# Decoder of two layers on one Trainium2 core: the value products of a self-attention unit issued in one block instead of two halves

## What is computed

```python
q = split_heads(_binlinear(x, Wq, bq))
k = split_heads(_binlinear(x, Wk, bk))
v = split_heads(_binlinear(x, Wv, bv))
att = jnp.einsum('bhtd,bhsd->bhts', q, k) * scale
att = jax.nn.softmax(att, axis=-1)
y = jnp.einsum('bhts,bhsd->bhtd', att, v)
y = y.transpose(0, 2, 1, 3).reshape(B, T, C)
return _binlinear(y, Wp, bp)
```

## Time and profile before

| | |
|---|---|
| median of 3 runs | 2285.22 us (2285.04 to 2290.65) |
| profiled execution, its own time | 2289.26 us |
| its span, first to last instruction | 2287.7 us |
| self-attention of layer 0, first to last step of the main stream | about 85 to 560 us |
| self-attention of layer 1, the same | about 921 to 1315 us |
| PE busy over the span | 76% |
| DVE busy | 60% |
| ACT busy | 47% |
| POOL busy | 37% |
| value products, L948 | 2048 records, 226.4 us busy |

### The profile page before, as it was taken

How to read it: one execution, slowest core, us unless ns; L and a number is a source line. 1 busy time by engine, 2 the same in 40 slices (tenths; PEclk the granted TensorE clock), 3 DMA queues, 4 the chain that set the end, 5 groups by cost and what they waited for, 6 DMA issues and landing times. The chain is left out here.

```text
span 2287.7 us, 35514 instructions
## 1 busy us (share of the span) xinstructions
PE 1738.8 (76%) x12206; PEld 875.7 (38%) x12222; DVE 1382.0 (60%) x3734; ACT 1080.9 (47%) x1482; POOL 841.4 (37%) x862
## 2 busy tenths in 40 slices
PE   4888888888688865677777745666656887999992
PEld 2122222222355542233333322323323554666661
DVE  2667777773478972566666543535447875555554
ACT  2366766766367962555555411121214563444441
POOL 3235554522477313577776430000002342222221
PEclk8589999999699986799998666668777998999996
DMA  4333332320100003344433014112112333222217
GB/s 95 61 66 61 58 62 50 49 27 1 67 1 1 1 4 56 53 63 57 56 48 48 2 28 58 25 35 38 37 30 95 124 121 106 63 61 61 59 53 234
DMA packets 117853, 126.58 MB, mean 55 GB/s; under 512 B 21684, under 2 KB 104116, under 8 KB 117652
## 3 DMA queue, kind: packets, MB, share of 16 engines
q1 hardware_dynamic: 106980, 101.94, 22.7%
q0 software_dynamic: 6480, 18.23, 2.1%
q10 hardware_dynamic: 4224, 4.19, 0.6%
HBM read 77.94 MB, written 45.16 MB: 54 GB/s over the span
## 5 line engine op out<-in xcount | busy, mean ns | idle before, releaser
L655 ACT ACTIVATE at_pexp<-ps 128x1024 f32<-128x1024 f32 (+3 forms) x480 | 385.8, 826 | 200.5 <-PE ps L888 199.4
L716 DVE TENSOR_REDUCE at_mx<-ps 128x1 f32<-128x512 f32 x512 | 324.0, 683 | 146.3 <-PE ps L895 144.3
L895 PE MATMUL ps<-at_ks,at_qs 48*128 48x512 f16 (+3 forms) x1024 | 291.6, 359 | 95.6 <-DVE at_mx L716 42.4
L182 PE MATMUL ps<-mo_wall,mo_xt 128*128 x1704 | 302.0, 327 | 1.1 <-DVE mo_xt L2316 0.6
L888 PE MATMUL ps<-at_qs,at_ks 50*128 50x512 f16 (+4 forms) x1024 | 253.8, 346 | 29.1 <-DMA at_qs<-at_mhl 23.2
L948 PE MATMUL ps<-at_pexp,at_vaug 128*32 128x512 f32 (+4 forms) x2048 | 226.4, 536 | 7.4 <-issue 6.3
L182 PEld LDWEIGHTS ps<-mo_wall,mo_xt 128*128 128x128 f16 x1704 | 161.1, 98 | 95.2 <-issue 4.3
L2073 POOL DMA_INDIRECT mo_yd<-mo_xn,mo_idu x71 | 68.1, 959 | 272.1 <-DVE mo_xn L2335 266.9
L718 DVE CUSTOM_DVE_ANT_0 at_junk<-ps,at_lmask 128x192 bf16<-128x192 f32 x384 | 115.4, 352 | 80.7 <-PE ps L895 79.6
L895 PEld LDWEIGHTS ps<-at_ks,at_qs 48*128 48x128 f16 x1024 | 75.4, 98 | 213.3 <-DVE at_mx L716 122.6
L888 PEld LDWEIGHTS ps<-at_qs,at_ks 50*128 50x128 f16 x1024 | 70.7, 98 | 174.6 <-issue 88.5
(11 more groups left out here) (397 smaller groups left out, 3873.2 us busy)
## 6 DMA issues: line engine op xcount, KB each, us to landing
at_qs<-at_scratch SPq DMA_DIRECT2D x96, 128.0 KB, 7.2
at_ks<-at_scratch SPq DMA_DIRECT2D x96, 128.0 KB, 7.8
mo_xr<-mo_xs SPq DMA_DIRECT2D x71, 136.0 KB, 2.3
at_scratch<-at_qkh SPq DMA_DIRECT2D x64, 128.0 KB
at_scratch<-at_qkl SPq DMA_DIRECT2D x64, 128.0 KB
x_qs<-x_qscratch SPq DMA_DIRECT2D x48, 128.0 KB
mo_stage<-in_m_gate SPq DMA_DIRECT2D x9, 512.0 KB, 3.7
mo_stage<-in_m_up SPq DMA_DIRECT2D x9, 512.0 KB, 4.6
```

The costliest lines, as they stand in the source:

```text
L182: last = nc.tensor.matmul(out, lhs, rhs, start=(n == 0), stop=(n == len(terms) - 1))
L655: last = act.activation(columns(pexp[:, U % 2, hh], at, n, stride, width), columns(banks(r, ST[S % 2], 2), at, n, stride, width), ACT.Exp, ...
L716: last = ve.reduce_max(out, score, AX.X)
L895: return nc.tensor.matmul(banks(r, MX[i % 2])[:, piece.at:piece.at + piece.n], qs[rows, (n // 2) % 2, h // 2, piece.idx * P:(piece.idx + 1 ...
```

## The change

In both rows of `PLACES` the first half of the value products goes one step later, to where the second half stands. The second half stays where it was. Nothing else is changed.

```diff
@@ -255,8 +255,8 @@
 PLACES = [
-    {"STATS": (-68, -62, -56, -54), "NORM": -52, "XT": (-47, -46), "QK": (-44, -39, -38, -37), "V": (-29, -18), "MT": (-4, 12), "TO": (37, 40, 41, 43), "YT": (53, 56), "OUT": (63, 65), "AV": (5, 6), "LEAD": 4, "BESIDE": (1.0, 1.0)},
-    {"STATS": (-50, -47, -47, -43), "NORM": -39, "XT": (-32, -30), "QK": (-27, -24, -23, -21), "V": (-19, -16), "MT": (-2, 9), "TO": (25, 25, 26, 29), "YT": (31, 35), "OUT": (40, 43), "AV": (6, 7), "LEAD": 2, "BESIDE": (1.0, 1.0)},
+    {"STATS": (-68, -62, -56, -54), "NORM": -52, "XT": (-47, -46), "QK": (-44, -39, -38, -37), "V": (-29, -18), "MT": (-4, 12), "TO": (37, 40, 41, 43), "YT": (53, 56), "OUT": (63, 65), "AV": (6, 6), "LEAD": 4, "BESIDE": (1.0, 1.0)},
+    {"STATS": (-50, -47, -47, -43), "NORM": -39, "XT": (-32, -30), "QK": (-27, -24, -23, -21), "V": (-19, -16), "MT": (-2, 9), "TO": (25, 25, 26, 29), "YT": (31, 35), "OUT": (40, 43), "AV": (7, 7), "LEAD": 2, "BESIDE": (1.0, 1.0)},
 ]
```

## The result

The changed kernel takes 2313.85 us (median of 4 runs, 2307.29 to 2317.58) against 2285.36 us before (median of 4): ratio 1.0116, 95% interval 1.0089 to 1.0143, that is 28.5 us slower. The forecast was 2303 us, 18 us slower, with a range to 2330. The profiled execution took 2314.0 us (span 2312.4), 24.7 us more than the one of before.

A forecast was written before the change was run, and what follows sets the result against it. PE and DVE were taken to bound the kernel by turns, through a two-bank ring. Layer 0 +9.5, layer 1 +3 and clock +5.5 made +18 us: 2307.3 on the profiled execution, 2303 us against the median; range 2288 to 2330.

The forecast's parts named there:

- The replay from rows: Layer 0: step times reworked unit by unit from the earlier trace, +1.5 us per batch, +9.5 us over the layer.
- DVE's two slots of work: Layer 0: two slots give DVE 1.2 us of reductions, while a joined block lasts 1.87 us.
- PE's wait of L895 for L716: Sign: PE's maxima stream waits longer for DVE's reductions, since it stands through two steps of scores; before, 27.7 us.
- Unit 0's gain of 0.3 us: Layer 1, unit 0: gains 0.3 us because its first block then need not wait for POOL's mask.
- the 3 us of the forecast: Layer 1's self-attention: +0.45 us per batch, times 7, taken as +3 us.
- I take one more fall in each of five batches, 5 x 1.1 = +5.5 us: Layer 0: PE's granted clock drops to about half once more in five batches, 1.1 us each.
- from one to two per batch: Sign for the clock term: stretches at granted clock 0.5 in layer 0 go from one to two per batch.
- the low end: Layer 0's clock term: chosen nearer no additional fall (0) than 24.5 us, because batch 3 had such a stretch without one.
- the clock falls too: Rival: 24.5 us instead of 5.5 for the clock, 2322 us, or some 2330 with layer 1; chance 0.2.
- Forecast at -1 us: Layer 0's last batch: no maxima, DVE no party, so joining gains 0.1 us per unit, -1 us.
- PE is the bound, and fewer switches win: Rival: each joined unit saves its full 0.21 us, 104 units, 22 us, giving 2263 us; chance 0.09.
- Absorbed: Rival: existing waits hide the loss in both layers and the clock stays; some 4 us, 2289 us; chance 0.15.

The follow-up runs named there:

- the kernel with filler in four steps: All of layer 0 joined, score matmuls repeated in steps 16, 17, 28 and 29 alone, against the kernel before: 2302.09 us, ratio 1.0083.
- the kernel with layer 1 alone: Value products joined in layer 1 only, layer 0 in halves as before, against the kernel before: 2283.34 us, ratio 0.9999.
- the joined kernel: Value products joined in layer 0, layer 1 as before, against the kernel before: 2314.51 us; with repeated score matmuls in thin steps, 2308.0 us.

## Why the prediction was right, and where it fell short

*The costs of joining, at full clock.* The distances between the first L888 of the steps, batch 3 of before against batch 2 of the kernel with filler in four steps, both at 1.00 throughout, give each unit's term (unit u from the start of step 4u+5 to that of step 4u+9, unit 7 from step 1 to step 5):

| unit of layer 0 | before, us | joined, us | difference | forecast |
|---|---|---|---|---|
| 7 | 7.38 | 6.99 | -0.39 | -0.5 |
| 0 | 8.12 | 8.01 | -0.11 | 0 |
| 1 | 6.52 | 6.50 | -0.02 | 0 |
| 2 | 6.34 | 7.05 | +0.71 | +0.6 |
| 3 | 8.39 | 8.53 | +0.14 | +0.25 |
| 4 | 6.34 | 6.83 | +0.49 | +0.45 |
| 5 | 9.25 | 9.51 | +0.26 | +0.2 |
| 6 | 7.25 | 7.82 | +0.57 | +0.5 |
| sum | 59.58 | 61.25 | +1.67 | +1.5 |

The six units without filler take the same in batch 3 of the changed kernel within 0.01 us; units 3 and 6 were clean only in the kernel with filler, and its eight extra matmuls are in their times. The replay from rows was right unit by unit, and with it its mechanism: the joined block outlasts DVE's two slots of work. In these two batches DVE's idle time in front of L716 rose from 11.8 to 15.3 us. One sign that the prediction named for this did not come: PE's wait of L895 for L716 did not rise but went from 5.6 to 5.0 us. And batch 3 of the changed kernel took 66.5 us, not the 61 to 62 that were to show the forecast right; that is the clock's part.

*Layer 1.* Right for unit 4: OUT starts 2.40 us after the block's start instead of 1.74, 0.66 us as forecast.

```profile
1112.65 1.51 PE L948 MATMUL ps<-at_pexp,at_vaug 128*32 128x192 f32 x32
1115.05 0.27 PE L182 MATMUL ps<-wh,at_yh 128*128 128x256 f16 x1 [0.89 <-ACT at_vaug L625]
```

The steps 2 to 4 of batches 2 to 5 take 8.29 us where they took 7.64 in the kernel before, and the kernel with layer 1 alone shows the same 8.29, so this loss is real. Unit 0's gain of 0.3 us did not come: the steps 6 to 8 of a batch take 4.36 us against 4.40. Whether the stretch lost the 3 us of the forecast can't be told: it is 4.3 us longer than in the profile of before and 1.7 us shorter than the longest of the profiles with layer 1 as before.

*The clock.* The step of the prediction that was mis-sized is "I take one more fall in each of five batches, 5 x 1.1 = +5.5 us". In batch 3 the steps of unit 3 took 11.32 us instead of 8.53 and those of unit 6 10.30 instead of 7.82; in batch 4 unit 0's took 9.64 instead of 8.01 as well. So there were two or three falls per batch in batches 3 to 5, and one that meets a whole joined block, with the matmuls around it, costs 1.6 us (3.4 us long, unit 0) to 2.8 us (6.8 us long, units 3 and 6) and not the 1.1 us that one fall of 3.4 us cost before. The sign "from one to two per batch" was right in direction and too low. Together that is 66.53 + 68.20 + 68.25 - 3 x 61.25 = 19.2 us, less the 2.2 us of falls that batches 4 and 5 had before: +17 us. The reason given for the low end, that batch 3 of before had such a stretch without a fall, was the wrong row to lean on: batches 2, 4 and 5 each had one (batch 4's is in the earlier trace rows). Of the units 2, 3, 4 and 6 that the prediction named as thinner, 3 and 6 fell in batches 3 to 5 and 2 only in batch 2; unit 0, which it did not name, fell in batches 4 and 5. The rival "the clock falls too" put 24.5 us on two further units in every batch.

*The last batch.* Forecast at -1 us, measured at +8.25: it ran at 1.00 before and at 0.87 now. With its halves back it ran at 0.87 too, so its own joined blocks are not needed for that; the cause is open. The sum had no term for the clock there.

Layer 0 in sum: 7 x 1.67 = 11.7 us for joining, +17 for the clock in batches 3 to 5, +8.25 for batch 7; batches 0 to 2 and 6 took 246.6 us against 248.1, that is 8.2 us less than joining alone would give, with 38 us at 0.5 against 62. That makes the 28.6 us measured, to 0.1; it is an account and not a check, since the 8.2 us are what was left over.

*How much of the hit is luck.* On the profiled execution the forecast was +18 us and the measured difference 24.7. The clock in batches 3 to 5 came out 11.5 us above the term for all batches, and batch 7 9.25 us above its own. Against that stand 8.2 us less in batches 0 to 2 and 6 and 8.0 us less in the cross-attention, for which the prediction had no terms; it said that everything outside the self-attentions would be unchanged. The direction and the size of joining at full clock were worked out; without these two, which nobody had forecast, the total would lie at 2330 us, the upper end of the range.

*The rivals.* "PE is the bound, and fewer switches win" was right in its price and wrong in its place: the block did become 0.14 us cheaper than two halves (1.86 against 2.00), but only units 7 and 0 turned out clearly shorter. "Absorbed" is wrong for layer 0. In layer 1 unit 4's loss was not absorbed on the spot, though the kernel with layer 1 alone can't be told from before.

## What to carry to other kernels

Where two engines feed each other through a ring of two, the length of the longest piece that one issues without feeding the other counts, not the sum: compare it with the work that the ring holds (here 1.87 us against 1.2 us), unit by unit, and only the places with other work beside them can take a longer piece. A longer piece also leaves a longer thin stretch beside it; if PE's clock falls behind thin stretches, the longest piece is what runs in it. Look in the trace of before at every place where the granted clock already falls once, and price each place that the change makes thinner with the whole piece at half clock.

## What the runs showed that was not expected

The cross-attention of layer 1, the same instructions in all of these kernels, took 392.6 us in the profile of before, at a granted clock of 0.73, and 384.6 us at 0.75 in that of the change; over the fourteen profiles here it ran from 382.0 to 392.6 us. Over 21, 16 and 31 runs the kernel before itself spread from 2271 to 2302 us. Layer 1's self-attention, with the same instructions, ran from 393.6 to 400.0 us over ten of them. A stage that an edit does not touch thus gets back or gives up as much as 10 us; what decides it was not tested. A difference in a total of this kernel can be trusted only with many runs or by the windows of its stages.

Matmuls that compute nothing new made a batch shorter: 48 more in batch 3 of the joined kernel, 3.7 us less.
